# Combining the expert results of a routed feed-forward layer: gathering all token rows in the last expert, or read, add and write back expert by expert

## The reference, cut to what matters

```python
logits = xf @ gate_w.T
probs = jax.nn.softmax(logits, axis=-1)
top_p, top_i = jax.lax.top_k(probs, K)                    # K = 2 of E = 8 experts
w = top_p / (jnp.sum(top_p, axis=-1, keepdims=True) + 1e-09)
capacity = int(CAPACITY_FACTOR * T / E)                   # 160
keep = (my_rank < capacity).astype(w.dtype)               # the first 160 of each expert and rank
comb = jnp.einsum('tk,tke->te', w * keep, oh.astype(w.dtype))
for e in range(E):
    y = silu(xf @ gate_proj_w[e].T) * (xf @ up_proj_w[e].T) @ down_proj_w[e].T
    out = out + comb[:, e:e + 1] * y
x = x + out
```

## Time and profile before

| | us |
|---|---|
| median of 3 runs | 1016.68 |
| lowest and highest of them | 1015.19, 1021.68 |
| the profiled execution, its own time | 1016.95 |
| the profiled execution, first to last instruction (span) | 1015.2 |

### The profile page before, as it was taken

The page is one execution under the profiler, slowest core; times in us unless marked ns, Lnnn a source line. Parts: engine busy times, 40 slices in busy tenths (PEclk is TensorE's granted clock), DMA queues, the critical chain, the costliest instruction groups (busy, mean ns, idle before and its releaser), DMA issues.

```text
span 1015.2 us, 14027 instructions
## 1 busy us (share of the span) xinstructions
PE 996.6 (98%) x5188; PEld 761.7 (75%) x5188; DVE 618.2 (61%) x1191; ACT 397.7 (39%) x638; POOL 210.7 (21%) x188
## 2 busy tenths in 40 slices
PE   7999999999999999999999999999999999999998
PEld 4886444444454558878888888898999999999997
DVE  6268443445656565896466766677666666656666
ACT  2332211213111143355667542534544544445441
POOL 2053400002000036454422124720000000000051
PEclk9999999999999999999999998999999999999999
DMA  9809589999999922023311100885664656645443
GB/s 290 316 1 389 242 341 422 406 410 396 411 390 408 375 81 82 1 86 112 109 46 34 32 2 6 303 264 174 183 196 139 204 168 184 186 154 181 153 143 135
DMA packets 45511, 206.91 MB, mean 204 GB/s; under 512 B 5536, under 2 KB 16032, under 8 KB 41232
## 3 DMA queue, kind: packets, MB, share of 16 engines
q1 hardware_dynamic: 40256, 187.95, 51.4%
q0 software_dynamic: 5200, 18.22, 5.1%
HBM read 190.04 MB, written 16.12 MB: 203 GB/s over the span
## 4 chain that ended last, share of the span: by engine, by line
PE 87%; DVE 8%; issue 1%; ACT 1%; DMA 1%; SPq 0%; POOL 0%; ACTq 0%; DVEq 0%
PE ps L476 28%; PE ps L892 20%; PE ps L908 10%; PE ps L640 9%; PE ps L611 8%; PE ps L470 1%; PE ps L588 1%; PE ps L621 1%; DVE stats L1278 1%; PE ps L644 1%; PE ps L933 1%; ACT w L1203 1%; PE ps L802 1%; DMA xr<-in_x 1%; PE ps L522 1%
## 5 line engine op out<-in xcount | busy, mean ns | idle before, releaser
L892 PE MATMUL ps<-x,w 128*128 128x320 f32 x1536 | 235.3, 309 | 2.2 <-DVE x L1861 1.1
L892 PEld LDWEIGHTS ps<-x,w 128*128 128x128 f32 x1536 | 230.0, 188 | 7.6 <-DVE w L1802 1.4
L1802 DVE TENSOR_TENSOR w<-big,w 128x1536 fp32r<-128x1536 f32 x64 | 112.4, 1758 | 80.7 <-ACT w L1203 80.1
L908 PE MATMUL ps<-w,hsplit 128*128 128x512 f32 x512 | 128.8, 393 | 0.0
L1203 ACT CAST w<-big 128x1536 fp32r<-128x1536 f32 x64 | 94.4, 1479 | 29.5 <-PE ps L908 29.5
L908 PEld LDWEIGHTS ps<-w,hsplit 128*128 128x128 f32 x512 | 93.3, 188 | 16.5
L611 PE MATMUL ps<-big 128*64 128x512 f32 (+2 forms) x512 | 98.2, 499 | 0.6 <-DVE s_stat L1458 0.6
L476 PE MATMUL ps<-xcT,u 128*128 128x512 f32 x432 | 98.2, 389 | 0.0
L476 PEld LDWEIGHTS ps<-xcT,u 128*128 128x128 f32 x432 | 81.0, 188 | 17.1 <-DVE xcT L1590 0.2
L640 PE MATMUL ps<-big 128*64 128x512 f32 x384 | 89.5, 599 | 2.1 <-DVE big L1437 0.5
L1232 ACT CAST hsplit<-big 128x320 fp32r<-128x320 f32 x64 | 29.4, 460 | 136.1 <-DVE big L1834 134.3
(11 more groups left out here) (337 smaller groups left out, 1528.6 us busy)
## 6 DMA issues: line engine op xcount, KB each, us to landing
big<-in_ctxT SPq DMA_DIRECT2D x16, 3202.0 KB, 16.6
big<-in_ctx SPq DMA_DIRECT2D x16, 3072.0 KB
big<-in_w_units SPq DMA_DIRECT2D x64, 768.0 KB, 4.3
big<-in_dense_units SPq DMA_DIRECT2D x41, 256.0 KB, 2.7
xs<-big POOLq DMA_DIRECT2D x1, 5120.0 KB, 17.4
big<-in_gate_units SPq DMA_DIRECT2D x12, 384.0 KB, 2.9
hr<-xs SPq DMA_DIRECT2D x28, 160.0 KB, 5.5
ys<-big POOLq DMA_DIRECT2D x7, 512.0 KB, 3.3
```

Of the source, the lines that this page charges most:

```text
L892: mm = nc.tensor.matmul(ps[:, 2 * part + f % 2, 0:SLOTS], wsplit[f % RING][w][:, c:c + P], xsplit[j][x][:, d, :], start=(d == 0 and w + x ...
L908: mm = nc.tensor.matmul(ps[:, 4 + s, :], x, w, start=(f == 0 and k == 0), stop=(f == FC - 1 and k == len(terms) - 1))
L1802: V.tensor_tensor(wsplit[f % RING][1][:], wraw[f % RING], wsplit[f % RING][0][:].bitcast(F32), ALU.subtract).then_inc(w_low, 1)
```

## The change

`ys`, the one-hot matrices of the last expert and the gathers at the end are gone. Instead the token's row in `out` is the accumulator:

- `out` has 320 more rows behind the 1,024 tokens; only the first 1,024 are the result. SP fills the spare ones at the start with a DMA from HBM to HBM (640 KB).
- As soon as the residual `xr` is there, SP writes it to `out` in three DMAs (`output_begun`), two behind the load of `slot_ids`, the third among the weight loads of expert 1.
- A table `tab` in HBM (8 bytes for each slot: token number + 1, weight) is zeroed, and once expert 0 has ended (`down_done` at FC) POOL scatters the tokens' 8-byte entries into it, 16 indirect DMAs of 128 entries. It waits for them and then loads the table turned over, slots on the partitions, in 3 DMAs (`slot_meta`).
- DVE waits for these loads (`slot_rows`) in expert 1 at f = 3, between the low part of the hidden values and the work on the next weight unit, and makes two lists: the row to read and the row to write of each slot (an empty slot reads row 0 and writes a spare row).
- For each expert n POOL gathers the 320 rows of `out` by these lists (3 DMAs), DVE adds the held result with its weight (`mix_held`, 3 operations) in the next expert at f = 4 (5 in expert 1, 3 in expert 7), and POOL scatters the rows back (3 DMAs). The gathers of n + 1 wait until the scatters of n have landed.
- The last expert's results are added straight from PSUM (`mix_last`, 4 operations), bank by bank in the order 0, 2, 1, in which its last `down` now fills them. SP waits for the last scatter.
- DVE's experts are written out one by one instead of partly in a hardware loop.

The diff, cut to its core:

```diff
+            sp.dma_start(out[T:T + SLOTS, :], a["x"][0:SLOTS, :]).then_inc(out_begun, 16)
...
+            output_begun(0, 4)
+            output_begun(4, 6)
...
-                for s in range(NS):
+                for s in LAST_ORDER if final else range(NS):
...
-                    if last:
-                        transpose_picks(f)
                     down(n, f, first, last and f == FC - 1)
...
-            for s in range(NS):
-                for i in range(4):
-                    last_rows(i, s)
-            for i in range(4, NT):
-                for s in range(NS):
-                    last_rows(i, s)
+            pe.wait_ge(y_evac, NS * NE)
...
+            def slot_rows():
+                dve.wait_ge(meta_in, 16 * NS)
+                ids = slot_meta[:, :, :, 0]
+                V.tensor_scalar(empty..., ids, 0.0, None, ALU.is_equal).then_inc(row_step, 1)
+                V.tensor_scalar(row_from..., ids, 1.0, 0.0, ALU.subtract, ALU.max).then_inc(rows_set, 1)
+                dve.wait_ge(row_step, 1)
+                V.tensor_tensor(spare..., empty..., spare_at..., ALU.mult).then_inc(row_step, 1)
+                dve.wait_ge(row_step, 2)
+                V.scalar_tensor_tensor(row_to..., ids, 1.0, spare..., ALU.subtract, ALU.add).then_inc(rows_set, 1)
...
+            def mix(n, s, y, signal):
+                m = slots_of(s)
+                return V.scalar_tensor_tensor(mixed_rows[0:m, s, :], y, slot_meta[0:m, n, s, 1:2], mixed_rows[0:m, s, :],
+                                              ALU.mult, ALU.add).then_inc(signal, 1)
+
+            def mix_held(n):
+                dve.wait_ge(mix_in, 16 * NS * (n + 1))
+                for s in range(NS):
+                    mix(n, s, held[0:slots_of(s), s, :], held_mixed)
+
+            def mix_last():
+                dve.wait_ge(mix_in, 16 * NS * NE)
+                for k, s in enumerate(LAST_ORDER):
+                    dve.wait_ge(last_done, k + 1)
+                    if s == NS - 1:
+                        dve.wait_ge(tail_high, NE)
+                        mix(NE - 1, s, ytail[0:LAST, :], mix_step)
+                        dve.wait_ge(mix_step, 1)
+                    mix(NE - 1, s, ps[0:slots_of(s), 4 + s, :], y_evac)
...
                     if f == 0 and not first:
-                        results_out(n - 1, 1 - j, half)
+                        hold_results(n - 1)
+                    if f == 3 and n == 1:
+                        slot_rows()
+                    if not first and f == (5 if n == 1 else 3 if last else 4):
+                        mix_held(n - 1)
                     if not (last and f + AHEAD >= FC):
                         split_low(n + (f + AHEAD) // FC, (f + AHEAD) % FC)
...
-                    if first and 2 <= f < 2 + NT // 2:
-                        pick_last_rows(2 * (f - 2))
-                    if first and f == FC - 2:
-                        pick_last_again()
...
             pool.wait_ge(idx_done, 3)
+            pool.wait_ge(down_done, FC)
             for i in range(NT):
                 for k in range(TOPK):
-                    G.indirect_dma_start(yg[i % 4][:, k, :], None, ys, ...gath...).then_inc(yg_in[i % 4], 16)
+                    G.indirect_dma_start(tab, ...scat[:, TOPK * i + k:TOPK * i + k + 1]...,
+                                         token_meta[:, i, k, :], None).then_inc(tab_out, 16)
+            pool.wait_ge(tab_out, 16 * NT * TOPK)
+            slot_tab = tab[0:TRASH, :].rearrange("(n r) w -> r n w", r=SLOTS)
+            for s in range(NS):
+                lo, hi = s * P, min(s * P + P, SLOTS)
+                pool.dma_start(slot_meta[0:hi - lo, :, s, :], slot_tab[lo:hi, :, :]).then_inc(meta_in, 16)
+            pool.wait_ge(out_begun, 16 * 4)
+            pool.wait_ge(rows_set, 2)
+            for n in range(NE):
+                if n:
+                    pool.wait_ge(mix_out, 16 * NS * n)
+                for s in range(NS):
+                    G.indirect_dma_start(mixed_rows[0:m, s, :], None, out, ...row_from...).then_inc(mix_in, 16)
+                for k, s in enumerate(LAST_ORDER if n == NE - 1 else range(NS)):
+                    pool.wait_ge(held_mixed if n < NE - 1 else y_evac, n * NS + k + 1)
+                    G.indirect_dma_start(out, ...row_to..., mixed_rows[0:m, s, :], None).then_inc(mix_out, 16)
```

## The result

The changed kernel takes 1023.52 us in the median (1020.67 to 1029.80, 20 runs), the kernel before on the same chips 1016.77 (1014.59 to 1023.65, 20 runs). The ratio is 1.0059, with a 95% interval of 1.0044 to 1.0075: slower, clear of noise, and within 1%. The forecast was 1020.6 and no change beyond 1%, as the difference of two large terms. Both terms are there. One of them, the gain at the end, came out a little over half as large.

A forecast was written before the change was run, and what follows sets the result against it. PE, busy 996.6 of 1015.2 us, was taken as the bound. Span 1015.2 - 10.9 (end) - 1.04 (expert 0) + 13.2 (stall) + 2.3 (clock) = 1018.8, plus 1.75 around it: 1020.6 us; 8-of-10 range 1010 to 1031.

The forecast's parts named there:

- The bound: Whole kernel: PE is busy 996.6 of 1015.2 us; added DVE work and traffic have room unless a wait holds DVE long.
- Rival 4: Additions expert by expert hold up DVE, if gathers and scatters land 25 us later than reckoned; chance 0.06 with other waits.
- Expert 0: PE's pause of 1.04 us between experts 0 and 1 goes, as the one-hot matrices are gone: a gain of 1.04.
- The stop of PE: In expert 1 PE stands still ahead of `down(4)` while DVE waits for the table: 13.2 us, bounds 6 and 22.
- Its landing, 2.0 later: The last of 16 table scatters, out at about 724.2, lands 2.0 us later, at 726.4; POOL waits for it.
- 160 per engine at 34 ns are 5.4 us: Table loads: 2,560 runs of 8 bytes, 160 per DMA engine at 34 ns each, take 5.4 us, until 733.0.
- Rival 2: Short runs cost nothing beyond the landing: DVE released at 731.4, stall 9.8, result 1017.2; chance 0.12 with other shorter stalls.
- rival 3: Short runs are dear, 68 ns or more each, with POOL's issues slowed: stall 22 us, result 1029; chance 0.18.
- The clock: Behind PE's stall in expert 1, some 4.6 us of full work run at half speed: 2.3 us lost.
- The end: Kernel end: 24 transposes of picks go (2.64 us), last rows are scattered sooner; gain 10.9 us, bounds 9 and 12.
- so the span would end: Last step at the kernel's end: 2.6 us from the last scatter's issue to landing, ending the span at 1004.2 to 1004.3.
- The early stages: Kernel start: filling the spare rows delays loads and zeroing of `xs`, hidden with 4.4 us to spare; at most 1 us.

## Why the prediction was right, point by point

- **The bound.** Right. PE is the bound in the experts, added DVE work and traffic there cost nothing: behind the stop, PE waits for nothing until the end, and DVE waits 0.4 us, once, for gathered rows. Rival 4 did not happen.
- **Expert 0.** Right: the 1.04 us are gone.
- **The stop of PE.** Right in place and mechanism, 12.1 us against 13.2, but by two errors that largely cancel, which is luck. The start (701.16) and the end of the last issue (724.1) of the scatters were as reckoned. The step "Its landing, 2.0 later" was mis-sized: POOL went on 4.7 us behind that issue (5.4 from its start to landing), and with entries of 512 bytes 1.6. That 8 bytes could cost more than 2 KB was put at nothing. (724.2 and 2.0 are 726.2, not 726.4.) The step "160 per engine at 34 ns are 5.4 us" was mis-sized the other way; from there to the semaphore there were 8.4 us in the forecast (726.4 to 734.8) and 4.2 in the run (728.84 to 733.04). These are the loads in the window from 728.8 to 733.1 us, by DMA queue (packets, MB, share of 16 engines):

```profile
q0 software_dynamic: 96, 0.02, 16.5%
```

  The 2,560 runs travel in under 96 packets, and 16.5% of 16 engines for 4.3 us are 11.4 us, 4.4 ns a run and 0.7 us for each engine, not 5.4. The rows gave a price for a packet, and I used it for a run. The last load landed 2.3 us after its start. On this the Trainium skill's fit (DMA: Bandwidth & Descriptors, Anatomy of one DMA), 2.0 us and next to nothing for the bytes, was nearer than my sum; for the short writes, at 5.4, it was too low by 3.4 us. Rival 2 was right that the loads' runs are cheap, rival 3 that the short stores are dear, and the two together made nearly the time of the forecast.
- **The clock.** Right that it falls, smaller: 1.7 us instead of 2.3 (the 4.6 us that the 2.3 rest on follow from no row). In 720 to 740 us the granted clock averages 0.77 and in the next 20 us 0.98; much of the time at 1.2 GHz lay in the stop itself, where PE had nothing to lose:

```profile
720.00:740.00 20.00, 7.86 (x38) 6.80 (x37) 5.59 (x11) 2.69 (x4) 9.43 (x10) 0.77 0.27 80
740.00:760.00 20.00, 20.00 (x120) 18.77 (x120) 15.09 (x25) 9.89 (x14) 8.03 (x6) 0.98 0.69 232
```

- **The end.** The picks' 2.64 us are gone as reckoned, and the last scatter landed 2.7 us after its start, against some 3.5 reckoned (the last issue, from 1000.45, ends at 1001.4 and not at 1001.6, a slip of 0.2). But the gain booked was 10.9 and is 6.1. The step that failed is the last: "so the span would end" at the landing. It ends when POOL has drained, 5.3 us later, a term that the sum doesn't have. The trace of before had the row of that drain, 8.85 us at 990.6. I didn't read it, since there it cost nothing; its cover, the last expert's matmuls, is what the change takes away by making POOL the last engine. These 4.8 us, less the 1.1 and 0.6 by which stop and clock were over-reckoned, are the 2.9 between forecast and result. With the end priced right and all else as forecast it would have been 1025.4, still within 1%. With the dear writes priced right too, some 2.5 us more, but not the cheap loads, it would have been 1027.9 and outside. So part of the agreement is that errors cancelled.
- **The early stages.** Hidden, as said: DVE's first wait for the energies is 12.69 us in both kernels.
- **What can be told.** The forecast took 1%, or 10 us, as the least that a measurement can tell from no change. Twenty runs of each kernel told 0.6%.

## What to carry to other kernels

A wait on an in-order engine costs what stands behind it: the release, plus the work owed to the next engine, less the cover in its queue; a step of cover was 5.35 us long here, and starting the producer earlier took away all of the 13.8 us. Ask of every moved step which engine is the last to finish, and read the rows of the block's end (drains, barrier) for that engine even if they cost nothing yet. A price per packet is not a price per run, and short writes and short reads have different prices.

## What the runs showed that I had not expected

- POOL's drain at the end of the program ends 4.0 us behind its last instruction, be it a memset or a plain DMA. Behind late gathers in the kernel before it ends 2.0 us behind the last landing; in the changed kernel it is 5.3 behind the last landing, and why it is longer there stays open.
- An indirect DMA that writes 128 entries of 8 bytes to HBM landed after 6.0 us (median of the 16; 2.6 to 10.0), one that writes 512 bytes each after 2.7 (2.2 to 6.2). The last one of 8 bytes took 5.4, with the DMA engines idle for the last 3.7 of them.
- A load of 1,024 runs of 8 bytes lands after 2.8 us: about 4.4 ns of one engine's time for a run.
